# Expert stage in units of two tiles, with the mixing tables made in eight pieces and no loops

## The reference

```python
k, v = xn @ key_w.T, xn @ value_w.T
r = sigmoid(xn @ recep_w.T)
# scan over time, per channel: carries aa, bb, pp (pp starts at -10000, aa and bb at 0)
p  = max(pp, tf + pp);  e1 = exp(pp - p);  e2 = exp(tf + pp - p)
wkv = (e1*aa + e2*v) / (e1*bb + e2 + 1e-6)
p2 = max(pp, td + pp);  e1b = exp(pp - p2); e2b = exp(td + pp - p2)
aa, bb, pp = e1b*aa + e2b*v, e1b*bb + e2b, p2
attn = (r * wkv) @ out_w.T
# mixture of experts: 8 experts, the best 2 of a softmax gate per token
expert_e = (silu(xn @ w1.T + b1) * (xn @ w3.T + b3)) @ w2.T + b2
shared   = (silu(xn @ ws1.T + bs1) * (xn @ ws3.T + bs3)) @ ws2.T + bs2
out = x + attn + gate1*expert_i1 + gate2*expert_i2 + shared
```

## Time and profile before

| | busy us | share of span |
|---|---|---|
| PE, matmuls | 471.3 | 87% |
| PE, weight loads | 381.2 | 71% |
| DVE | 428.3 | 79% |
| ACT | 239.9 | 44% |
| POOL | 260.9 | 48% |

### The profile page before, as it was taken

How to read it: one execution, slowest core, us unless ns; L and a number is a source line. 1 busy time by engine, 2 the same in 40 slices (tenths; PEclk the granted TensorE clock), 3 DMA queues, 4 the chain that set the end, 5 groups by cost and what they waited for, 6 DMA issues and landing times. The chain is left out here.

```text
span 539.1 us, 10721 instructions
## 1 busy us (share of the span) xinstructions
PE 471.3 (87%) x2624; PEld 381.2 (71%) x2625; DVE 428.3 (79%) x963; ACT 239.9 (44%) x543; POOL 260.9 (48%) x311
## 2 busy tenths in 40 slices
PE   1885094999899999999999868899999999999997
PEld 1332042787788878777877757687889888888887
DVE  7797993578878888888888835998978888797964
ACT  1677251366556656565655555314232324242321
POOL 2000003535656666666566546787656573747200
PEclk9998555899989999999999997999999999999999
DMA  7999201383333334333433327527171625254011
GB/s 246 387 362 319 96 0 29 107 276 113 125 101 113 107 116 127 108 118 115 125 109 108 109 76 230 189 89 233 43 212 57 198 82 171 84 170 131 26 39 41
DMA packets 58553, 73.95 MB, mean 137 GB/s; under 512 B 6848, under 2 KB 47552, under 8 KB 58528
## 3 DMA queue, kind: packets, MB, share of 16 engines
q1 hardware_dynamic: 52048, 55.94, 31.0%
q0 software_dynamic: 6480, 17.70, 12.2%
HBM read 45.39 MB, written 28.18 MB: 136 GB/s over the span
## 5 line engine op out<-in xcount | busy, mean ns | idle before, releaser
L834 POOL DMA_INDIRECT xg<-xn_rows,picked x71 | 71.2, 1003 | 56.0 <-POOL picked L831 38.7
L1319 POOL DMA_INDIRECT yg<-expert_rows,rows x64 | 71.4, 1115 | 23.6 <-issue 17.1
L898 PE MATMUL ps_g<-w_hi,x_hi 128*128 x142 | 57.5, 405 | 0.8 <-issue 0.8
L898 PE MATMUL ps_g<-w_lo,x_hi 128*128 x142 | 56.9, 401 | 0.0
L898 PE MATMUL ps_g<-w_hi,x_lo 128*128 x142 | 56.9, 401 | 0.0
L831 POOL COPY picked<-tile_tok 128x1 int32 (+1 forms) x71 | 14.3, 201 | 86.5 <-POOLq L317 82.5
L1350 PE MATMUL ps_w<-col_hi,s_hi 128*128 128x512 f32 x128 | 51.0, 399 | 1.6 <-DVE res L1545 1.0
L971 ACT ACTIVATE act<-ps_g 128x256 f32<-128x256 f32 x71 | 27.2, 383 | 52.0 <-PE ps_g L901 48.4
L1351 PE MATMUL ps_w<-col_lo,s_hi 128*128 128x512 f32 x128 | 50.2, 392 | 0.0
L1352 PE MATMUL ps_w<-col_hi,s_lo 128*128 128x512 f32 x128 | 50.2, 392 | 0.0
L1452 ACT ACTIVATE sact<-ps_w,vec_b 128x512 f32<-128x512 f32 x32 | 22.0, 687 | 59.6 <-PE ps_w L1352 47.6
(11 more groups left out here) (192 smaller groups left out, 1412.2 us busy)
## 6 DMA issues: line engine op xcount, KB each, us to landing
expert_rows<-y SPq DMA_DIRECT2D x71, 128.0 KB
table<-mix_tables SPq DMA_DIRECT2D x16, 384.0 KB, 5.2
xin<-x SPq DMA_DIRECT2D x16, 256.0 KB, 4.2
xn_rows<-xn SPq DMA_DIRECT2D x16, 256.0 KB, 4.7
xn_columns<-xT SPq DMA_DIRECT2D x8, 512.0 KB, 4.5
col<-xn_columns SPq DMA_DIRECT2D x8, 512.0 KB, 7.3
mix_tables<-coef SPq DMA_DIRECT2D x16, 256.0 KB
res<-x SPq DMA_DIRECT2D x16, 256.0 KB
```

Of the source, the lines that this page charges most:

```text
L834: pool.indirect_dma_start(out=xg[a.buf(NG)][:], out_offset=None, in_=xn_d[:, :], in_offset=bass.IndirectOffsetOnAxis(ap=picked[a.buf(NG)][ ...
L898: nc.tensor.matmul(out, x[:, k, :], w[:, ds(e, 1), k, cols].rearrange("p o n -> p (o n)"), start=(k == 0 and n == 0), stop=False)
L1319: pool.indirect_dma_start(out=yg[a.buf(2)][:, k, q, :], out_offset=None, in_=y_d[:, :], in_offset=bass.IndirectOffsetOnAxis(ap=picked[a.bu ...
```

## The change

The expert stage works in 36 units of two tiles (`DUOS`; the last has one tile). Each `gather` makes one copy of two columns of row numbers and then two indirect DMAs; `turn_x`, `turn_h`, `up` and `down` do both tiles in a row; each eviction by ACT or DVE covers both, 512 columns instead of 256. To fit the eight PSUM banks, `ps_x` and `ps_h` have one buffer of two tiles instead of two of one; `act1` and `hid` have one as well. So `turn_x(a)` waits for `cut_x(a-1)`, and `turn_h(a)` for `cut_h(a-1)`. The four `xg` buffers hold two tiles each. DVE does `hidden` right behind `gate`, ahead of `cut_h`.

A piece of the tables is 256 time steps, there are 8, one in four units (the same rate per tile as before). The work is in place: the relu and exp results in `firsts` and `decay`, the reciprocal in `den`, the coefficients in `firsts`, which has two buffers. One of them, and `dif`, borrow the space of two operands of the mixing stage, whose loads move to the end of the stage. The reciprocals are four of 128 elements behind three different units. POOL does `factors` behind the second and `denominator` behind the third gather of four.

Nothing loops: all index arithmetic is done when the kernel is built. A table is stored and loaded in contiguous lines, and a step of the mixing stage loads its table with one DMA instead of two. The rest of the mixing stage and the routing stage are as before.

The core of the diff (removed lines are left out where the listing above shows them):

```diff
-ROUNDS = -(-TILES // 4)
-REST = TILES - 4 * (ROUNDS - 1)
+DUOS = -(-TILES // 2)
 EPS = 1e-5
-PIECE = 128
+PIECE = 256
...
-            y = [sb(f"y{b}", [P, C], F32, experts, "right") for b in range(2)]
+            y = [sb(f"y{b}", [P, 2, C], F32, experts, "right") for b in range(2)]
...
         NG = 4
+        picked = [sb(f"picked{b}", [P, 2], I32) for b in range(NG)]
+        xg = [sb(f"xg{b}", [P, 2, C], F32) for b in range(NG)]
+        x_hi = [sb(f"x_hi{b}", [P, 2, KC, P], F32R) for b in range(2)]
...
+        act1 = sb("act1", [P, 2, FF], F32)
+        hid = sb("hid", [P, 2, FF], F32)
...
+        dif = raw_vr[:].rearrange("p k n -> p (k n)").rearrange("p (n k t) -> p n k t", n=2, k=KC)
...
+        firsts = [col0[:].rearrange("p k n -> p (k n)").rearrange("p (n k t) -> p n k t", n=2, k=KC),
+                  sb("firsts", [P, 2, KC, PIECE], F32)[:]]
...
+        ps_x = bank("ps_x", [P, 2, KC, P])
+        ps_g = [bank(f"ps_g{b}", [P, 2, 2 * FF]) for b in range(2)]
+        ps_h = bank("ps_h", [P, 2, KC, P])
+        ps_y = [bank(f"ps_y{b}", [P, 2, C]) for b in range(2)]
...
+        def tiles(a):
+            return min(2, TILES - 2 * a)
...
                 def store(a):
+                    sp.wait_ge(c_yc, a + 1)
+                    sp.dma_start(y_d[2 * a * P:(2 * a + n) * P, :].rearrange("(t p) c -> p t c", p=P),
+                                 y[a % 2][:, 0:n, :]).then_inc(y_stored[a % 2], 16)
...
+                for a in range(DUOS + 1):
+                    if a > 0:
+                        store(a - 1)
+                    v, r = divmod(a, 4)
+                    if r == 1 and v < NPIECE:
+                        store_decay(v)
+                    if r == 2 and 0 < v <= NPIECE:
+                        store_coef(v - 1)
+                    if 0 < a <= len(loads):
+                        sp.dma_start(*loads[a - 1]).then_inc(c_ld, 16)
+                    if a == 4 * LAST_V + 1:
+                        sp.wait_ge(t_sides, NPIECE)
+                        sp.dma_start(raw_vr[:], wvr).then_inc(c_vr, 16)
+                    if a == 4 * LAST_V + 3:
+                        assert (LAST_V - 1) % 2 == 0
+                        sp.wait_ge(t_cst, LAST_V * 16)
+                        sp.dma_start(col0[:].rearrange("p k n -> p (k n)"), columns).then_inc(c_col, 16)
...
                 def gather(a):
+                    b, n = a % NG, tiles(a)
+                    at_least(pool, c_tx, a - NG + 1)
+                    nc.gpsimd.tensor_copy(picked[b][:, 0:n], tile_tok[:, 2 * a:2 * a + n]).then_inc(c_idx, 1)
+                    pool.wait_ge(c_idx, a + 1)
+                    for t in range(n):
+                        pool.sem_inc(c_go, 1)
+                        pool.indirect_dma_start(
+                            out=xg[b][:, t, :], out_offset=None, in_=xn_d[:, :],
+                            in_offset=bass.IndirectOffsetOnAxis(ap=picked[b][:, t:t + 1], axis=0)
+                        ).then_inc(c_gath[b], 16)
+                def denominator(v):
+                    own = OwnIn(pool, t_pool, At(0, v, NPIECE), 2)
+                    f = firsts[v % 2]
+                    pool.wait_ge(t_bb, v + 1)
+                    pool.wait_ge(t_exp_f, v + 1)
+                    at_least(pool, t_coef, v)
+                    own.link(nc.gpsimd.tensor_tensor(den[:], f[:, 0], s_b[:, :, 0:PIECE], ALU.mult))
+                    own.link(nc.gpsimd.tensor_tensor(den[:], den[:], f[:, 1], ALU.add))
-                    pool.sem_inc(c_go, 1)
                     nc.gpsimd.tensor_scalar(den[:], den[:], 1e-6, 2.0, ALU.add, ALU.mult).then_inc(t_den, 1)
+                def factors(v):
+                    f = firsts[v % 2]
+                    pool.wait_ge(t_rec, v + 1)
+                    nc.gpsimd.tensor_tensor(f, f, den[:, None].broadcast_to([P, 2, KC, PIECE]),
                                             ALU.mult).then_inc(t_coef, 1)
+                for a in range(NG):
+                    gather(a)
+                for a in range(DUOS):
+                    v, r = divmod(a, 4)
+                    if a + NG < DUOS:
+                        gather(a + NG)
+                    if r == 1 and 0 < v <= NPIECE:
+                        factors(v - 1)
+                    if r == 2 and v < NPIECE:
+                        denominator(v)
...
                 def turn_x(a):
+                    pe.wait_ge(c_gath[a % NG], a // NG * 32 + tiles(a) * 16)
+                    at_least(pe, c_xlo, a)
+                    for t in range(tiles(a)):
+                        for k in range(KC):
+                            mm = nc.tensor.transpose(ps_x[:, t, k, :], xg[a % NG][:, t, k * P:(k + 1) * P], ident[:])
                     mm.then_inc(c_tx, 1)
...
+                es = {}
+                turn_x(0)
+                turn_x(1)
+                es[0] = experts(0)
+                up(0, es[0])
+                turn_x(2)
+                es[1] = experts(1)
+                up(1, es[1])
+                for a in range(DUOS):
+                    if a + 2 < DUOS:
+                        es[a + 2] = experts(a + 2)
+                    turn_h(a)
+                    if a + 3 < DUOS:
+                        turn_x(a + 3)
+                    if a > 0:
+                        down(a - 1, es.pop(a - 1))
+                    if a + 2 < DUOS:
+                        up(a + 2, es[a + 2])
+                down(DUOS - 1, es.pop(DUOS - 1))
...
                 def cut_x(a):
+                    if a >= DUOS:
+                        return
+                    n = tiles(a)
+                    act.wait_ge(c_tx, a + 1)
+                    at_least(act, c_g, a - 1)
+                    nc.scalar.activation(x_hi[a % 2][:, 0:n], ps_x[:, 0:n], ACT.Copy).then_inc(c_xhi, 1)
...
+                def halves(v):
+                    f = firsts[v % 2]
+                    act.wait_ge(t_dif, v + 1)
+                    at_least(act, t_cst, (v - 1) * 16)
+                    at_least(act, t_est, v * 16)
+                    at_least(act, t_bb, v)
+                    nc.scalar.activation(f[:, 1], dif[:, 0], ACT.Relu, scale=-1.0)
+                    nc.scalar.activation(f[:, 0], dif[:, 0], ACT.Relu)
+                    nc.scalar.activation(decay[:], dif[:, 1], ACT.Relu).then_inc(t_sides, 1)
+                def exps(v):
+                    f = firsts[v % 2]
+                    act.wait_ge(t_sides, v + 1)
+                    nc.scalar.activation(decay[:], decay[:], ACT.Exp, scale=-1.0).then_inc(t_exp, 1)
+                    if v == 0:
+                        act.wait_ge(t_feed, 2)
+                    for c in range(KC):
+                        nc.scalar.activation(f[:, 0, c, :], f[:, 0, c, :], ACT.Exp, scale=-1.0, bias=feed[:, c:c + 1])
+                    nc.scalar.activation(f[:, 1], f[:, 1], ACT.Exp, scale=-1.0).then_inc(t_exp_f, 1)
...
+                halves(0)
+                cut_x(0)
+                cut_x(1)
+                silu(0)
+                cut_x(2)
+                for a in range(DUOS):
+                    v, r = divmod(a, 4)
+                    silu(a + 1)
                     cut_h(a)
+                    cut_x(a + 3)
+                    if a > 0:
+                        result(a - 1)
+                    if r == 0 and v < NPIECE:
+                        exps(v)
+                    if r == 3 and v < LAST_V:
+                        halves(v + 1)
+                    if a == DUOS - 3:
+                        act.wait_ge(c_vr, 16)
+                        nc.scalar.activation(vr[1][:], raw_vr[:], ACT.Copy).then_inc(c_whi, 1)
+                    if a == DUOS - 2:
+                        act.wait_ge(c_col, 16)
+                        nc.scalar.activation(col[1][:], col0[:], ACT.Copy).then_inc(c_whi, 1)
+                result(DUOS - 1)
...
+                def invert(v, i):
+                    c, h = divmod(i, 2)
+                    part = den[:, c, h * (PIECE // 2):(h + 1) * (PIECE // 2)]
+                    dve.wait_ge(t_den, v + 1)
+                    ins = nc.vector.reciprocal(part, part)
+                    if i == 2 * KC - 1:
                         ins.then_inc(t_rec, 1)
...
+                grown(0)
+                differences(0)
...
+                for a in range(DUOS):
+                    v, r = divmod(a, 4)
+                    gate(a + 1)
+                    hidden(a + 1)
+                    cut_h(a)
+                    cut_x(a + 3)
+                    if r == 0 and 0 < v <= NPIECE:
+                        invert(v - 1, 1)
+                        invert(v - 1, 2)
                     if r == 1:
+                        if 0 < v <= NPIECE:
+                            invert(v - 1, 3)
+                        if v < NPIECE:
+                            scan_b(v)
+                    if r == 2 and v < LAST_V:
+                        grown(v + 1)
+                    if r == 3:
+                        if v < LAST_V:
+                            differences(v + 1)
```

(37 more changed lines are left out.)

377 lines of the change are left out of this document (115 added, 262 removed).

## The result

The changed kernel took 552.9 us (median of 4 runs, 551.3 to 555.0) against 540.6 us (539.8 to 542.2) for the kernel before: a ratio of 1.023 with a 95% interval of 1.018 to 1.027, so slower beyond the noise. Forecast were 538.5 us and a range of 528 to 550. The profiled run took 553.4 us with a span of 551.7, where before it was 540.8 and 539.1.

- the expert stage: PE's last matmul ends at 327.3 instead of 319.8 (+7.6)
- the switch to the mixing stage: PE stands 7.5 us instead of 5.3 (+2.3)
- the mixing stage: 551.7 - 334.9 = 216.8 us instead of 214.1 (+2.7)

The account below looks back on a forecast made before the run. The prediction took a ring through POOL and DVE, 12.68 us per four tiles, as the bound. From 540.8 us it took 1.8 (expert stage) and 0.5 (mixing) to reach 538.5; own range 534 to 542, with rivals 528 to 550.

Parts of the forecast that it names:

- Start: Expert stage's first units on PE: four gathers needed before `up(0)`; unit 0 begins at 106.2 us, unit 5 at 133.4.
- Units of two tiles: PE in the expert stage: same matmuls and transposes, so 5.78 us a unit, no more and no less.
- evictions: DVE and ACT, 512 columns instead of 256: 2.4 instead of 2.6 us a unit on DVE; nothing taken as gain.
- POOL's order: POOL's queue in the expert stage makes gathers late for PE: period P of eight tiles 25.2 us, against 25.36 before.
- Landing: Expert stage, from a gather's DMA instruction end to PE: 1.8 and 2.2 us in the trace, taken as 2.0.
- The clock falls at the gather wait: Rival, PE in expert stage: seven waits of 1.4 to 2 us; if all lower the clock, 10 us: 548; chance 0.07.
- the worst port waits: DVE and POOL sharing SBUF: upper bound 2.6 us, scans of 1.3 at two places; placed above the range's 550.
- No loops: PE's code in the expert stage: first loop return cost 1.74 us inside POOL's chain, so nothing gained; straight code not slower.
- End: Expert stage's end: PE ends at 318.0, gain 1.8 us; POOL's cuts hidden by 5.2 us, 2.3 if not.
- The rival on the switch: Expert to mixing stage: if loops cause the 5.2 us from PE's end, up to 4 go: 534.5 us; chance 0.13.
- Mixing: Mixing stage: one contiguous table load instead of two saves at most DVE's 0.50 us wait; 0.5 taken.
- The port rival: Expert stage: scans hold up POOL's copy and denominator in full, 2.0 us a period instead of 0.7: 547.6 us; chance 0.28.

Follow-up runs that it names:

- p: Kernel a with each eviction of 512 columns on ScalarE and VectorE done as two of 256 with one signal: 526.7 us.
- a: Changed kernel with GpSimd's `factors` and `denominator` both moved behind the fourth gather of a turn: 531.3 us, ratio 0.983.
- d: Changed kernel with coefficients of pieces 1 to 7 stored for 16 of 128 partitions only (64 KB instead of 512 KB each): 549.6 us.
- e: Kernel before, with `factors` behind the four gathers of a turn instead of behind the first: 545.8 us, ratio 1.009.
- b: Changed kernel with the expert stage's last two subtractions (vr_lo, col_lo) on VectorE instead of GpSimd: 545.0 us, ratio 1.006 to the kernel before.
- c: Kernel before, with the expert stage's last two subtractions (vr_lo, col_lo) on VectorE instead of GpSimd: 537.3 us, ratio 0.993.
- s: Changed kernel with GpSimd's first bias in the mixing stage waiting for VectorE's first hidden instruction: 548.9 us, ratio 1.015.
- f: Changed kernel with 64 float32 matmuls of one column more on TensorE while it waits for the first gather: 572.4 us.
- h: Changed kernel with the load of row_b2 (128 KB) issued with unit 8 instead of unit 6: 552.3 us.
- k: Changed kernel with 64 small one-pass matmuls more on TensorE while it waits for the first gather: 561.0 us (2 runs).

## Why the prediction was wrong

The profiled run took 553.4 us, 14.9 over the forecast. Of these, 9.4 are in the expert stage (+7.6 against -1.8), 2.3 in the switch and 3.2 in the mixing stage (+2.7 against -0.5).

- *Start* (106.2 and 133.4): measured 106.32 and 133.57. Right.
- *Units of two tiles* (5.78, no more and no less): right; *evictions* (nothing): right by p.
- *POOL's order* (P = 25.2): right in four periods of seven, and a shows that the order was the whole price: 13.6 us of plain waits. A part of the agreement is luck: in the period from 186.62 the landing of gather(4v+7) took 2.29 instead of 2.0 us, and gaps of 0.30 instead of 0.42 and an earlier start of `factors` gave that back.
- *Landing, "I take 2.0"*: the step that failed. It was read from gathers that had the DMA engines to themselves. Measured from the DMA instruction's end to PE are 2.7 to 3.0 us for gather(4v+6) (2.3 to 2.5 with the store cut to 64 KB, by d), 2.3 to 2.4 for gather(4v+7), and 4.8, 3.7 and 4.6 in units 7, 20 and 31. In unit 7 it met row_b2 and PE's instruction packet, in unit 20 the packet, in unit 31 the store and something that stays open. The transfer is hidden no longer, so all that shares its engines counts.
- *The clock falls at the gather wait* (a rival, 0.07, "against it: the wait is split over two units"): it fell three times, where single waits were longer than I had them. I let a rival and a term share a cause, and gave them chances as if they were independent. The two together are the 8.9 us, and with them 552.9 lies outside the range, whose upper end I had put at the worst port waits.
- *No loops* ("nothing is gained", "straight code is not slower"): not slower where it runs, but its 22 packets meet gathers. Nor is nothing gained once the gathers come in time: e keeps PE's loop and loses 10.8 us at its returns, and a, without loops, has no such gap. I had asked whether PE would stand for its code, and not what the code's transfer would stand in the way of.
- *End* ("I let the 5.2 us hide them, 2.3 if they don't"): the price of the other branch was right (2.3 measured), the choice wrong. I measured the switch from PE's end; b and c show that it counts from POOL's. The pair 318.86 and 325.07 was in the trace of before. The rival on the switch looked at loops, and had the wrong reason for the same rows.
- *Mixing* (-0.5): 0.6 came, part_v starting 5.9 us into the stage instead of 6.5. But with the single table load SP had also issued the four loads of x 4.1 us into the stage instead of 8.7, so GpSimd's first bias no longer waited 2.12 us for their rows, and came before part_a: +3.3, and s takes 4.0 back.
- The port rival was wrong in its place: 0.7 a period was enough in the expert stage. POOL's two copies took 0.58 and 0.46 us there instead of 0.18, and its denominator 3.5 as forecast. (Its threshold has a slip: 0.3 times 7 is 2.1 and not 2.3; nothing hangs on it.) The collision that cost was in a stage that I had taken as given.

Open: what else unit 31's gather waits for (1.81 us remain in d), why DVE and POOL alternate at their ports in one run and not in another, why the returns of PE's loop got longer in e, and what besides the length of a wait decides whether the clock falls.

## What to carry to other kernels

Ask of every wait in a queue which later instruction behind it is free to go, and put that first: here two steps of GpSimd's order, moved behind the last gather of a turn, were worth 22 us, more than all else together. The same move cost the kernel before 5 us, since the returns of TensorE's loop then came to the fore. A transfer that an engine waits for has the price of everything that shares its DMA engines, the loading of instructions too. And read the switch between stages from the engine whose distance is the same in every trace.

## What the runs showed of the hardware

- A switch of stages took 6.20 to 6.22 us from GpSimd's last instruction in every trace where that set it, and 0.9 us from ScalarE's where it didn't (c). Before the expert stage GpSimd had been idle for 82 to 83 us and the switch took 0.3 us.
- A 16 KB packet of instructions took 1.25 us of one DMA engine's time beside unit 20; on average it is 1.2 (0.3% of 16 engines over 551.7 us, for 22 packets).
- Of 17 waits of 2.0 to 3.5 us for gathered rows (the changed kernel, b, d, f, h, k and s), 14 were followed by a low clock, and the unit was 1.5 to 2.9 us longer than 5.78 and the wait; those of 2.08 in d, 2.17 in b and 2.68 in f were not. Of shorter ones 1.86 in s (unit 20) was, and 1.71 in f, 1.80 in k and 1.81 in d were not. Of six gaps of 1.72 to 1.78 us at returns of PE's loop three were (1.74 in the kernel before, 1.78 and 1.73 in e), and three were not (1.78 in c, 1.73 and 1.72 in e). In this stage none of 1.25 us or less was.
- 64 float32 matmuls of one column took 27.4 us at the 0.50 clock (128 records), and 64 one-pass ones of two columns 13.8 us (64 records): the same 0.21 us a record.
- Two instructions of GpSimd back to back kept one of VectorE out for both (6.13 us for 1.21), and who came first there decided 3 to 5 us of the whole.
